# Attention loop of a two-layer block: LayerNorm two batches ahead, transposes ahead of the down projection, projection pieces and router products at other places

## The reference

```python
xn = layernorm(x)
s  = attention(xn, w_qkv, w_out)                      # causal, 16 heads of 16
g  = silu((silu(xn @ wg.T) * (xn @ wu.T)) @ wd.T)     # 768 hidden units
x  = x + s * g
xn = layernorm(x)
s  = hyena(xn)                                        # short filter, two long filters by FFT
g  = silu(top2_of_20_experts(xn))                     # router: gelu(xn @ wg1) @ wg2, softmax, top 2
x  = x + s * g
```

## Time and profile before

| | before |
|---|---|
| median of 3 runs | 1171.7 us (1168.32 to 1173.43) |
| the profiled execution's own time | 1162.91 us |
| its span, first to last instruction | 1161.2 us |
| mean granted TensorE clock | 0.918 |
| TensorE busy | 995.3 us (86% of the span) |
| VectorE busy | 703.3 us (61%) |
| ScalarE busy | 482.2 us (42%) |
| POOL busy | 408.5 us (35%) |

### The profile page before, as it was taken

One profiled execution on the slowest core, in us unless ns is written; L12 is line 12 of the kernel. 1 busy time (PEld: TensorE's weight loads), 2 busy tenths in 40 slices (PEclk: granted clock), 3 DMA queues, 4 the chain that ended last, 5 costly groups with the idle time before them and its releaser, 6 DMA issues. The chain is left out here.

```text
span 1161.2 us, 19301 instructions
## 1 busy us (share of the span) xinstructions
PE 995.3 (86%) x5936; PEld 759.8 (65%) x5936; DVE 703.3 (61%) x1456; ACT 482.2 (42%) x887; POOL 408.5 (35%) x604
## 2 busy tenths in 40 slices
PE   0758899999989998998999998985599989999995
PEld 0645586676577577667667666564466668888884
DVE  4235367556556647547547645646357437989997
ACT  1313543544444454454463553454122234544441
POOL 6111321361260351351252352243200026687770
PEclk9987997997998899799799998798699999999998
DMA  4653463543543353353263453029467654233331
GB/s 145 138 90 94 67 150 133 76 100 127 81 104 127 57 128 127 54 112 145 39 117 123 85 92 107 2 85 342 149 204 218 204 177 146 91 122 115 124 95 36
DMA packets 88554, 137.22 MB, mean 118 GB/s; under 512 B 10867, under 2 KB 64307, under 8 KB 86324
## 3 DMA queue, kind: packets, MB, share of 16 engines
q1 hardware_dynamic: 70148, 101.41, 35.3%
q0 software_dynamic: 6144, 16.79, 4.7%
q10 hardware_dynamic: 12208, 18.35, 4.6%
HBM read 79.88 MB, written 55.57 MB: 117 GB/s over the span
## 5 line engine op out<-in xcount | busy, mean ns | idle before, releaser
L1441 DVE TENSOR_REDUCE Mneg<-PS 128x2 f32<-128x1024 f32 (+2 forms) x192 | 194.9, 1043 | 100.7 <-PE PS L984 100.6
L1221 ACT ACTIVATE PT<-PS 128x512 f32<-128x512 f32 (+1 forms) x384 | 170.2, 537 | 179.5 <-PE PS L1009 179.2
L1669 POOL TENSOR_TENSOR idle_p<-neghalf 128x1 f32<-128x1 f32 x128 | 24.9, 195 | 391.2 <-ACT PT L1221 391.2
L1009 PE MATMUL PS<-qs,ks 96*128 96x512 f32 (+3 forms) x512 | 140.7, 392 | 14.1 <-DMA qs<-mrow 11.3
L980 PE MATMUL PS<-ks,qs 96*128 96x256 f32 (+3 forms) x512 | 136.4, 378 | 4.4 <-DVE xnT L1367 2.1
L1009 PEld LDWEIGHTS PS<-qs,ks 96*128 96x128 f32 x512 | 100.0, 215 | 41.3 <-ACT PT L1221 17.1
L811 PE MATMUL PS<-xnT,Wgu 128*128 128x512 f32 x384 | 100.8, 406 | 4.8 <-ACT V L1166 2.4
L1022 PE MATMUL PS<-PT,V 128*32 128x512 f32 (+3 forms) x1024 | 89.6, 497 | 13.2 <-POOL PT L1675 13.2
L1825 PE MATMUL PS<-Wes,xbT 128*128 x336 | 97.9, 401 | 3.3 <-issue 2.0
L1675 POOL TENSOR_SCALAR_AFFINE_SELECT PT<-PT 128x256 f32<-128x256 f32 x256 | 99.6, 413 | 0.0
L980 PEld LDWEIGHTS PS<-ks,qs 96*128 96x128 f32 x512 | 87.9, 222 | 17.7 <-issue 7.4
(11 more groups left out here) (226 smaller groups left out, 1759.0 us busy)
## 6 DMA issues: line engine op xcount, KB each, us to landing
qs<-qk_parts SPq DMA_DIRECT2D x96, 128.0 KB
ks<-qk_parts SPq DMA_DIRECT2D x96, 128.0 KB
xb<-slots_in SPq DMA_DIRECT2D x84, 128.0 KB, 2.4
slots_out<-yb ACTq DMA_DIRECT2D x28, 384.0 KB, 3.1
qk_parts<-qhl SPq DMA_DIRECT2D x16, 512.0 KB, 2.6
qk_parts<-khl SPq DMA_DIRECT2D x16, 512.0 KB, 2.7
xn2T_parts<-xn2T SPq DMA_DIRECT2D x8, 1024.0 KB, 4.8
xT<-xn2T_parts ACTq DMA_DIRECT2D x7, 1024.0 KB, 4.9
```

Source lines behind the costliest of these rows:

```text
L1009: last = pe.matmul(PS[:, 4 + n, col:col + T - P * kt], ks[:, hd, P * kt:P * kt + P], qs[:, hd, P * kt:T], start=True, stop=True)
L1221: act.activation(PT[:, g % 2, j, 512 * n:512 * n + width], PS[:, 4 + n, 0:width], ACT.Exp, scale=SCALE).then_inc(S["exped"], 1)
L1441: dve.tensor_reduce(out=Mneg[:, 0, qt, heads[0]:heads[-1] + 1], in_=all_of, op=ALU.max, axis=AX.X, negate=True).then_inc(S["maxed"], 1)
```

## The change

The LayerNorm of batch b+2 is computed by VectorE in batch b, between `route_choice` and `ranks`, with POOL's power ahead of the masks of group 3; only batch 1's stays where it was. x of batch b+2 is loaded at the start of batch b. The transposes of x-hat go ahead of the down projection in batches 1 to 6, and the splits of x-hat with them. The query and key pieces stand between the units of group 0, one earlier for the last two; the router's hidden product follows the last unit and goes to bank 7; the router's logits follow the second unit of group 1. The rows of maxima are written with one transfer in place of two. The first gate piece goes ahead of the row maxima of group 3, one more place in step 4 is dropped, the buffers of hidden tiles 0 and 1 change places, and the first two tiles of the value projection go to both sides of the last values product. The loops of VectorE, POOL and SyncE end one batch earlier, and that batch is written out.

```diff
-        BANK = (0, 2, 4, 6, 4, 6)
+        BANK = (2, 0, 4, 6, 4, 6)
+        COUNT_BANK = (1, 3)
@@ SyncE
                 def load_x(b):
-                    at_least(sp, S["ln_done"], b)
+                    at_least(sp, S["ln_done"], NT * b)
@@
                 def stack(b, g):
+                    if g == 0:
+                        sp.wait_ge(S["spilt"][0], 32 * (b + 1))
                     at_least(sp, S["st_ps"], 48 * (b - 1) + 12 * (g + 1))
-                    if g % 2 == 0:
-                        sp.wait_ge(S["spilt"][g // 2], 32 * (b + 1))
+                    if g == 2:
+                        sp.wait_ge(S["spilt"][1], 32 * (b + 1))
@@
                 def rows_of_maxima(b, g):
                     sp.wait_ge(S["mrow_sb"], NG * b + g + 1)
-                    for r in range(2):
-                        sp.dma_start(f(qs[M0 + r:M0 + r + 1, GH * g:GH * g + GH, :]),
-                                     mrow[GH * NT * r:GH * NT * (r + 1), :]).then_inc(S["m_in"], 16)
+                    sp.dma_start(f(qs[M0:M0 + 2, GH * g:GH * g + GH, :]), mrow[:, :]).then_inc(S["m_in"], 16)
@@
-                    if not last:
+                    if first:
                         load_x(b + 1)
-                    else:
+                    if ahead:
+                        load_x(b + 2)
+                    if last:
                         load_filter()
@@ TensorE
                 def transposed_x(b):
                     pe.wait_ge(S["ln_done"], NT * (b + 1))
-                    at_least(pe, S["h32_sb"], NF * b)
+                    if not (isinstance(b, int) and b == 0):
+                        pe.wait_ge(S["h32_sb"], NF * b - 1)
@@
+                GATES = {(NG - 1, NU): ((0,), (0,)), (NG, 1): ((0,), (1,)), (NG, 2): ((1,), (0,)),
+                         (NG, NU): ((1,), (1,))}
+                COUNT_AT = (4, 5)
@@ attention
+                            if s == NG + 1 and u == 0 and not last:
+                                project_v(b + 1, (0,))
                             if u == 1 and 2 <= s:
                                 values(b, s - 2)
-                            if s == NG and u == 5 and not first:
-                                counts(b - 1, 3)
+                            if s == NG + 1 and u == 2 and not last:
+                                project_v(b + 1, (1,))
+                            if s == 1 and u == 1 and not first:
+                                route_logits(b - 1)
+                            if s == NG and u == COUNT_AT[last] and not first:
+                                counts(b - 1, COUNT_BANK[last])
                             if s == NG and u == NU and not first:
                                 pe.wait_ge(S["counts_in"], b)
-                            if s == NG and u in (1, 2, 4, 6) and not last:
-                                n = (1, 2, 4, 6).index(u)
-                                gate_up(b + 1, (n // 2,), (n % 2,))
+                            if (s, u) in GATES and not last:
+                                gate_up(b + 1, *GATES[s, u])
@@ sequence
                     gate_up(b, range(EARLY, NF))
+                    if not first and not last:
+                        transposed_x(b + 1)
                     down(b, first)
-                    if not last:
+                    if first:
                         transposed_x(b + 1)
                     unit(b, 0, 0)
-                    if not first:
-                        route_hidden(b - 1, b + 1)
                     if last:
                         filter_step(0)
                     unit(b, 0, 1)
-                    qk_tiles = iter(()) if last else iter(range(4))
-                    for u in range(2, NU + 1):
-                        if not last and u != 4:
-                            project_qk(b + 1, (next(qk_tiles),))
+                    for u in range(2, NU):
+                        if not last:
+                            project_qk(b + 1, (u - 2,))
                         if last and u == 4:
                             filter_step(1)
-                        if u < NU:
-                            unit(b, 0, u)
+                        unit(b, 0, u)
                     if last:
                         filter_step(2)
+                    if not first:
+                        route_hidden(b - 1, b + 1)
                     maxima_as_rows(b, 0)
-                    if not first:
-                        route_logits(b - 1)
                     attention(b, first, last)
-                    if not last:
-                        project_v(b + 1, (0, 1))
@@ ScalarE: split_x ahead of gate_of_output, route_hidden after split_qk, route_exps at s == 2
@@ VectorE, attention
                         for u in range(NU):
                             maxima(b, g, u)
+                            if g == 1 and u == 2 and not first:
+                                route_logits(b - 1)
@@
                         for part in range(4):
                             route_choice(b - 1, part)
+                    if ahead:
+                        norm(b + 2, NORM_X)
+                    if not first:
                         for part in range(2):
-                            ranks(dve, b - 1, 3, part)
+                            ranks(dve, b - 1, COUNT_BANK[last], part)
@@ VectorE, sequence
-                    if not last:
-                        norm_stats(b + 1, NORM_X)
-                        norm_variance(b + 1, NORM_X)
-                        norm_rows(b + 1, NORM_X)
+                    if first:
+                        norm(b + 1, NORM_X)
+                    if not last:
+                        split_x(b + 1)
                     if not first:
                         split_x1(b - 1)
-                    if not last:
-                        split_x(b + 1)
@@ POOL
-                def masks(b):
+                def masks(b, ahead):
                     for g in range(NG):
+                        if g == NG - 1 and ahead:
+                            power(b + 2, veps, rstd, "ln_var", "ln_std")
@@ VectorE, POOL and SyncE
-                with dve.Fori(1, B - 1) as b:
+                with dve.Fori(1, B - 2) as b:
                     sequence(b)
+                sequence(B - 2, ahead=False)
```

More of the change, by code:

```diff
@@ L784, in _ @@
                 sequence(0, first=True)
-                with sp.Fori(1, B - 1) as b:
+                with sp.Fori(1, B - 2) as b:
                     sequence(b)
+                sequence(B - 2, ahead=False)
                 sp.wait_ge(S["xn2T_out"], 16 * (B - 2))
-                sequence(B - 1, last=True)
+                sequence(B - 1, last=True, ahead=False)
                 sp.wait_ge(S["xn2T_out"], 16 * (B - 1))
@@ L1232, in attention @@
                 def attention(b, first, last):
-                    if not first:
-                        route_exps(b - 1)
                     for s in range(1, NG + 2):
+                        if s == 2 and not first:
+                            route_exps(b - 1)
                         if s == NG + 1 and not last:
@@ L1281, in sequence @@
                         act.activation(Fwd[:, HI, :, :], st_f[:, :, :], ACT.Copy).then_inc(t_hi, 1)
-                    if not first:
-                        route_hidden(b - 1)
                     if last:
@@ L1479, in first_group @@
                     maxima(b, 0, 1)
-                    qk_tiles = iter(range(4))
-                    for u in range(2, NU + 1):
-                        if not last and u != 4:
-                            split_qk(b + 1, (next(qk_tiles),))
-                        if u < NU:
-                            maxima(b, 0, u)
-                        if u == NU - 1:
-                            parts_of_maxima(b, 0)
+                    for u in range(2, NU):
+                        if not last:
+                            split_qk(b + 1, (u - 2,))
+                        maxima(b, 0, u)
+                    parts_of_maxima(b, 0)
                     if last:
@@ L1490, in first_group, with attention @@
                     rows_of_maxima(b, 0)
-                    if not first:
-                        route_logits(b - 1)
-                def attention(b, first, last):
+                def attention(b, first, last, ahead):
                     for g in range(1, NG):
@@ L1536, in residual, with sequence @@
                     dve.tensor_tensor(xres[:, :, :], xres[:, :, :], G[:, :, :], ALU.add).then_inc(S["x1_sb"], 1)
-                def sequence(b, first=False, last=False):
+                def sequence(b, first=False, last=False, ahead=True):
                     gated(b, 3)
@@ L1689, in sequence @@
                                            ).then_inc(t_lo, 1)
-                    masks(b)
+                    masks(b, ahead)
                     if last:
@@ L1716, in _ @@
                 sequence(0, first=True)
-                with pool.Fori(1, B - 1) as b:
+                with pool.Fori(1, B - 2) as b:
                     sequence(b)
```

(3 more changed lines are left out.)

26 lines of the change are left out of this document (17 added, 9 removed).

## The result

The changed kernel takes 1138.28 us (median of 4 runs, 1136.37 to 1142.21) against 1170.01 us for the kernel before (4 runs, 1168.14 to 1173.43): a ratio of 0.975 with a 95% interval of 0.971 to 0.978. The forecast was 1128, with a range of 1104 to 1157. The profiled execution took 1136.37 us, span 1134.6, mean granted clock 0.924; before 1162.91, 1161.2 and 0.918.

What follows compares the result with a forecast made beforehand. TensorE's own stream plus small waits (6.7 us a batch), and its clock, bound the kernel. Profiled 1162.9 - 19.3 (waits) - 24 (clock) = 1119.6; with the same distance to the median, 1128 us, range 1104 to 1157.

Steps and rivals of the forecast that it cites:

- Waits: Sum of the gains from TensorE's shortened waits over all batches, apart from the clock: 19.3 us, bounds 10 and 24.
- (c): Value projection ahead of the last value product: half a piece fills the 0.94 us mask wait; -0.75 us a batch.
- (a): Transposes of x-hat ahead of the down projection fill waits for hidden tiles 4 and 5; -1.09 us per looped batch.
- (b): Edge between head groups 0 and 1: earlier copy, one transfer for two; 4.07 to 3.15 us, -0.9 us.
- (d): Gate piece before the row maxima of group 3, buffers swapped: what is gained ahead is waited for behind; 0.
- (e): LayerNorm two batches ahead fits VectorE's 4.85 us wait between choice and ranks; 0, bounds 0 to +1.0 us a batch.
- Rival D: Slower: the LayerNorm ends late and TensorE waits for `counts_in`, masks held too; 1183 us, chance 0.04.
- the first of the two signs of being wrong: A wait for VectorE stands before the gate piece at the end of group 3.
- (g): TensorE's clock: half of 130 us at 1.2 GHz goes, at 0.37 us each; -24 us, ends none and 48.
- The second sign: The clock's mean over the batches is still 0.91, where 0.95 or more was expected.
- Rival A: The clock stays as it is and only the waits are gained; 1152 us, chance 0.20.

Runs made afterwards that it cites:

- e3: Changed kernel with two transfers of the row maxima again in place of the single one; 1150.5 us, ratio 0.984 to the kernel before.
- e2: Changed kernel with transposes and splits of x-hat behind the down projection again; 1154.7 us, ratio 0.990 to the kernel before.
- e4: Changed kernel with the first two value projection tiles behind the attention again; 1120.8 us, ratio 0.958 to the kernel before.
- e7: Changed kernel with gate pieces and count at their old places in group 3 and step 4; 1133.7 us, ratio 0.968 to the kernel before.
- e8: Kernel before with only the LayerNorm two batches ahead, with its load; 1167.6 us, runs from 1136.9 to 1169.3.
- e5: Changed kernel plus seven unread products a batch in the two waits between groups 0 and 1, batches 0 to 6; 1116.2 us, ratio 0.955.
- e6: Kernel before plus thirteen unread products a batch in its two waits between groups 0 and 1, batches 0 to 6; 1133.2 us, ratio 0.969.
- e10: e5 with POOL's low part of hidden tile 2 kept behind VectorE's residual addition; 1114.5 us, ratio 0.964 to the kernel before.
- e12: e10 plus five more unread products before the router's counts, and VectorE's wait for the scatters moved ahead of the next x1 norm; 1107.9 us, ratio 0.947.
- e1: The changed kernel run again without any edit; 1136.1 us, ratio 0.975 to the kernel before.

## Why the prediction was right, and which term was off

Direction and range held; the time came 10 us above the number.

- **Waits, -19.3: got -19.0, by luck.** Two errors in the parts cancel: (c) gave less than nothing for 0.75, and (a), with the moves that it allows, gave about as much more. Of the 2.6 us of a batch, (b) has 0.84 and the rest have 1.8, where 1.09 + 0.75 were forecast.
- **(b), -0.9 an edge: right in size, and in most of its reasons.** 0.84 us came, 0.53 of them from the earlier copy and issue. The single transfer is the smaller part: undone, it costs 0.15 us at the edge (e3), and not the 0.6 us of a second issue.
- **(a), -1.09 a batch, was not the whole of its part.** The step said that tile 5's wait would shrink to 0.4; it stayed at 0.91. What it also missed is that the new place of the router's product takes the cover from the split of x-hat, so that without (a) 1.86 us of new wait appear (e2). I had priced the parts as if they were independent.
- **(c), -0.75 a batch, was wrong: +0.2 to +0.8.** The row showed 0.94 us of TensorE waiting, and the step asked only which work of TensorE could fill it. It did not follow the end of the batch, which hangs on a chain: last mask, values product, ScalarE's copy and hidden rows, POOL's two low parts, six scatters of 1.27 us each and their landing, VectorE's product. Behind the values product TensorE arrives sooner and waits for that. And only 0.45 us of the mask wait were left (e4), so that a piece of 0.85 us delays the values product, which the chain goes through.
- **(d) and (e), 0 each: right**, by e7 and e8, within the error of 2 us. The LayerNorm fits as the sum said. The timeline of the kernel after, step 4, shows how closely:

```profile
314.14 1.02 POOL L1673 TENSOR_TENSOR rstd<-veps,neghalf 128x4 f32<-128x4 f32 x1 [5.24 <-DVE veps L1367]
...
315.26 1.92 DVE L1375 TENSOR_SCALAR xn<-xin,mv,rstd 128x256 f32<-128x256 f32 x4 [1.21 <-POOL rstd L1673]
...
318.03 1.20 PE L816 MATMUL PS<-xnT,Wgu 128*128 128x512 f32 x4 [0.20 <-DVE next_row L668]
```

The rows take 1.92 us, not 1.38, beside POOL's masks, and TensorE waits 0.20 us for `counts_in`. Rival D's mechanism is there, 0.20 us large where it needed more than 2.8. It is also the first of the two signs of being wrong that I had named, a wait for VectorE before the gate piece at the end of group 3's heads, and too small to matter.

- **(g), the clock, -24, is the term that failed:** about -10 by the runs (27 us x 0.37), 12.7 in the first pair of medians, and 6 in the profiled pair (190 to 173 us in all). The place was right: e5 and e6 show that the low stretches come from the thin stretch between groups 0 and 1. The size was a halving chosen between two ends, and shorter waits there (0.49 and 0.40 us for 0.48 and 1.24) were not enough. The second sign, a loop mean still at 0.91, says so. Filled waits were enough in either kernel, for the looped batches. Rival A's sum (1152) less these 10 us gives 1142; 1138 was measured.
- The Trainium skill ("TensorE: Matmul & The Clock Gate", "HAM oscillation — how this bites in real kernels") puts such falls down to long idle gaps. By that section, e5 and e6 should have changed nothing; filling waits of at most 1.24 us took 59 and 88 us out. The measurement decides, against that section.

## What to carry to other kernels

Before a wait of the busiest engine is priced as a gain, follow the end of the stage back along every engine: here VectorE's product started 3.3 us after POOL's last scatter in before, after and e4, so time won on TensorE behind the values product was lost again, and the piece put ahead of that product made the chain longer. A wait that ends within 0.1 us of a second one must be taken away together with it, or it seems worthless (e10, then e12). And where the granted clock falls again and again behind the same thin stretch, try a few unread products in its waits first: a few lines gave 36 us in the old order and 20 to 22 in the new.

## What the runs showed that I had not expected

- The clock fell behind a stretch whose waits were all under 1.3 us, and unevenly: the same program had 3 and 17 us at 1.2 GHz in neighbouring batches (e1), and 116 or 208 us in whole executions (e8). Through all of it 1 us at 1.2 GHz costs 0.37 us here, over 80 executions. The last batch, which I left unfilled, still has 25 us of it in e12.
- The residual addition of VectorE (two operands in SBUF) takes 1.23 us alone and 1.53 or 2.16 when POOL's 1.3 us subtraction runs beside it. It ends 1.1 us after POOL's in each case (334.81 and 335.91 after), as if it worked only when POOL was done. The Trainium skill ("SBUF — State Buffer", "Who interferes with whom") says that such a VectorE instruction contends with a GpSimd instruction that reads SBUF, over ports that one of them holds alone; the rows agree, and e10, which keeps them apart, has 1.23 in all eight.
- One of POOL's scatters costs that engine 1.27 us from issue to issue (0.96 and a gap of 0.30), and the last of eight lets its waiter go 3.20 us after its issue begins (e10). Once that wait was elsewhere (e12), the same product followed at 2.38.
